# A six-layer attention stack and a quantised feed-forward on one core: the steady order of all five queues written anew, implied waits dropped, filler products dropped

## The chip, the cores and the metric

One core of a Trainium2 chip runs the whole program in one launch. The metric is the device time in microseconds (us); three runs of the kernel before gave 1197.34, 1201.46 and 1201.83, median 1201.46.

## What is computed

The input is x, eight sequences of 1024 rows of 128. For each sequence b, six vectors come from a condition vector: `mod = silu(c) @ wmod`, split into sa, ca, ga, sb, cb, gb.

```
h = layernorm(x) * (1 + ca) + sa
for i in range(6):                      # the attention stack, h is its x
    xn = layernorm(x, ln1)
    q = softmax(xn @ wq, head dim); k = softmax(xn @ wk, rows); v = xn @ wv
    x = (q @ (k.T @ v)) @ wo + bo + x   # linear attention, 8 heads of 16
    xn = layernorm(x, ln2)
    x = leaky_relu(xn @ w1) @ w2 + x    # hidden width 512
x = x + ga * h
x = x + gb * fp4_ffn(layernorm(x) * (1 + cb) + sb)   # inner width 352
```

`fp4_ffn` rounds inputs and weights in blocks of 16 to the values of a 4-bit float and computes `silu(gate) * up` and the down product. All is float32.

## The kernel before

**Items.** An item is one sequence in one layer: 48 items, number i, layer i // 8. A sequence's 1024 rows lie as 128 partitions x 8 tiles of 128. Per item TensorE does product_k (4 products of 512 columns, fp32, line 556), product_q (16 of 128 columns, fp32, line 568), product_z (k against the normalised rows, 16 fp32, line 577), context and context_out (2 fp32 each, lines 585 and 591), attend (16 fp32, line 598), eight first_mlp pieces (each three float16 products of 512 columns, lines 612 to 614: high x high, low x high, high x low), and eight second_mlp pieces (each twelve float16 products of 128 columns, lines 627 to 629). In the record an fp32 product shows as two passes; the counts here are of passes.

**Who does what.** ACT (ScalarE) takes the hidden pieces out of PSUM (copy_hidden, line 880), splits them into high halves (line 889), scales the normalised rows (lines 850 and 861) and does the exponentials. DVE (VectorE) does statistics (lines 1097 and 1103), softmax maxima and sums, 32x32 block transposes (lines 1184, 1198, 1207) and the additions into x_all. POOL (GpSimd) does the low halves (hidden_low, line 1785; second_norm_low, line 1777), the roots and part of the scaling. SP (SyncE) issues every DMA of the loop: round trips through DRAM that finish the transposes of n, q and k (send_..., fetch_...), and turn_hi and turn_lo (lines 331 and 336), two DMA transposes that bring the split rows of item i into norm2_hi and norm2_lo, which the first_mlp pieces of item i read.

**One buffer.** norm2_hi and norm2_lo exist once. So turn_hi(i) and turn_lo(i) wait `hidden_done >= PIECES * i`: all eight first_mlp pieces of item i - 1 must be over. first_mlp(i, 0) waits for the landing of both. Between the last piece of item i - 1 and the first piece of item i lies what TensorE does in the meantime.

**Orders.** Each engine runs a function `items(v)` for v = 0, 1, 2, ...; a line `if on(v - 4): first_mlp(v - 4, 6)` means that in step v the engine does this piece of item v - 4. The engines' queues are in order, so these lists, written out by hand, are the schedule; semaphores only hold it together. Lines with `v == n` are the opening (weights are folded and split, the first items are transposed by TensorE) and the start of the feed-forward, whose units (16 of half a sequence) begin in steps 48 to 53 and then run in `ffn_phase`. `round_weights` and `prepare_gates` are one extra DVE operation in each of steps 10 to 26 and 27 to 44. `keep_warm` (line 522) is TensorE's filler in steps 0 to 3: products of 256 columns that nobody reads.

Of the kernel before, what the change touches and what calls it, by code (L numbers as in the profile page):

```python
# [37 lines left out]
def adaln_block(nc, x, ln1_w, ln1_b, wq, wk, wv, wo, bo, ln2_w, ln2_b, w1, w2,  # L38
# [31 lines left out]
    with ctx:  # L70
# [208 lines left out]
        def _(sp):  # L279
# [143 lines left out]
            for v in range(ITEMS + 3):  # L423
                items(v)
# [24 lines left out]
        def _(pe):  # L449
# [99 lines left out]
            def product_k(i):  # L549

                pe.wait_ge(norm1_t_ready, i + 1)
                pe.wait_ge(wk_ready, 16 * (i // B + 1))
                w = wk_s[:, i // B % 2 * D:i // B % 2 * D + D]
                after(pe, ctx_o_ready, i - 1)
# [5 lines left out]
            def product_q(i):  # L560

                pe.wait_ge(norm1_t_ready, i + 1)
                pe.wait_ge(wq_ready, 16 * (i // B + 1))
                after(pe, q_shifted, i)
# [16 lines left out]
            def context(i):  # L581
                pe.wait_ge(z_t_ready, i + 1)
                pe.wait_ge(wv_ready, 16 * (i // B + 1))
# [3 lines left out]
            def context_out(i):  # L587
                pe.wait_ge(ctx_t_ready, i + 1)
                pe.wait_ge(wo_ready, 16 * (i // B + 1))
# [11 lines left out]
            def first_mlp(i, n):  # L601
# [14 lines left out]
            def second_mlp(i, t):  # L616
# [3 lines left out]
                if t % TH == 0:  # L620
                    pe.wait_ge(weights_ready, 2 * DEPTH)
                    pe.wait_ge(hidden_lo_ready, 2 * i + h + 1)
                    after(pe, x_ready, 2 * (i - 1) + h + 1)
# [37 lines left out]
            def product_gate(u, t):  # L661
                pe.wait_ge(f_x_q_t_ready, u + 1)
# [4 lines left out]
            def product_up(u, t):  # L667
                pe.wait_ge(f_x_q_t_ready, u + 1)
# [4 lines left out]
            def turn_hidden(u, t):  # L673
                if u == 0:
                    pe.wait_ge(x_ready, 2 * ITEMS - 1)
                pe.wait_ge(f_hid_q_ready, u + 1)
# [7 lines left out]
            def product_down(u):  # L684
# [3 lines left out]
                pe.wait_ge(f_x1_ready, u + 1)  # L688
# [29 lines left out]
            def items(v):  # L718
                if v == 0: turned_bias_rows()
                if v == 0: hidden_bias_cols()  # L720
                if v == 0: output_bias_rows()
                if v == 0: keep_warm(mlp0_bank, 18)
                if v == 0: turn_first_n(0)
                if on(v - 2): context_out(v - 2)
                if v == 2: keep_warm(mlp0_bank, 10)
                if v == 3: keep_warm(mlp0_bank, 16)
                if on(v - 4): first_mlp(v - 4, 6)
                if on(v - 4): first_mlp(v - 4, 7)
# [1216 lines left out]
```

## Time and profile before

| | |
|---|---|
| median of three runs | 1201.46 us |
| the profiled execution | 1198.31 us |
| its span in the trace | 1196.6 us |
| busy of the span: PE, POOL, DVE, ACT | 94%, 91%, 90%, 87% |
| instructions | 30119 |
| fillers, line 522 | 172 products, 22 us busy |

A share of busy time is a mean over three stages: the opening (to about 160 us), the steady items, and the feed-forward at the end (from about 970 us). PE's busy time has modelled ends: for TensorE read the distance from one start to the next. The row PEclk gives the granted clock, 9 or 1.00 being the full 2.4 GHz and half of it 1.2 GHz.

### The profile page before, as it was taken

What the parts mean: (1) busy time and instruction counts of PE and PEld (TensorE: products, weight loads), DVE (VectorE), ACT (ScalarE), POOL (GpSimd) and SP (SyncE); (2) the same over time, 40 slices, a digit from 0 to 9 for tenths busy, and PEclk for the clock granted to TensorE, in tenths of its full rate; (3) what the DMA queues carried; (4) which work ended last, traced back from release to release, by engine and by line L of the source; (5) the groups of instructions that cost most, each with busy time, mean ns of one, the idle gap of its engine ahead of it and who ended that gap; (6) DMA issues with size and microseconds to landing.
All of it is one profiled execution on the core that took longest, in us unless ns stands there. A gap on an engine that the chain in (4) does not pass through costs nothing.

```text
span 1196.6 us, 30119 instructions
## 1 busy us (share of the span) xinstructions
PE 1130.7 (94%) x9722; PEld 865.7 (72%) x9722; DVE 1074.4 (90%) x2885; ACT 1035.2 (87%) x1776; POOL 1091.4 (91%) x920
## 2 busy tenths in 40 slices
PE   7787999999999999999999999999999988999996
PEld 5575777777777777777778777777787755565664
DVE  7899989989999999999999999999987589999972
ACT  5687999999999999999999999999999886767662
POOL 4889999999999999999999999999999988999762
PEclk8798999999999999999999999999999999999998
DMA  8121877777667776687776776766777420110000
GB/s 308 36 71 53 234 187 224 195 195 223 193 195 214 196 216 194 180 224 187 216 201 197 216 206 183 221 190 204 208 193 218 108 71 18 36 37 36 18 19 36
DMA packets 213864, 190.22 MB, mean 159 GB/s; under 512 B 113392, under 2 KB 192080, under 8 KB 213712
## 3 DMA queue, kind: packets, MB, share of 16 engines
q1 hardware_dynamic: 213712, 188.31, 55.3%
q8 instruction: 81, 1.33, 0.5%
q14 instruction: 71, 0.58, 0.2%
HBM read 87.06 MB, written 76.02 MB: 136 GB/s over the span
## 4 chain that ended last, share of the span: by engine, by line
PE 50%; POOL 24%; issue 15%; DVE 6%; ACT 2%; DMA 1%; SPq 1%; DVEq 0%; POOLq 0%; ACTq 0%
POOL hidden L1785 10%; POOL rows_split L1777 4%; PE pair_mlp L556 4%; PE pair_mlp L577 4%; PE pair L598 4%; PE pair L568 4%; PE ring_pair L612 3%; PE ring_pair L614 3%; PE ring_pair L613 3%; PE mlp L696 3%; PE pair_mlp L670 3%; POOL arena L1758 2%; POOL arena L1791 2%; PE pair_mlp L681 2%; PE mlp L629 2%
## 5 line engine op out<-in xcount | busy, mean ns | idle before, releaser
L1785 POOL TENSOR_TENSOR hidden<-hidden 128x2048 f16<-128x2048 f32 x92 | 376.3, 4090 | 0.0
L880 ACT ACTIVATE hidden<-ring_pair,hidden_bias 128x512 f32<-128x512 f32 x384 | 245.6, 686 | 26.1 <-PE ring_pair L614 26.0
L889 ACT ACTIVATE hidden<-hidden 128x2048 f16<-128x2048 f32 x96 | 183.3, 1909 | 19.9 <-PE mlp L629 16.1
L1097 DVE BATCH_NORM_STATS2 bn<-x_all 128x6 f32<-128x128 f32 x896 | 184.2, 278 | 5.3 <-POOL x_all L1737 2.0
L1711 POOL TENSOR_TENSOR rstd<-ve,minus_half 128x8 f32<-128x8 f32 x104 | 170.7, 1641 | 0.0
L850 ACT ACTIVATE arena<-x_all,nmr,rstd 128x128 f32<-128x128 f32 x384 | 157.7, 494 | 0.0
L612 PE MATMUL ring_pair<-arena,halves 128*128 128x512 f16 x384 | 146.0, 380 | 3.4 <-ACT hidden L880 1.7
L614 PE MATMUL ring_pair<-arena,halves 128*128 128x512 f16 x384 | 146.0, 380 | 0.0
L613 PE MATMUL ring_pair<-arena,halves 128*128 128x512 f16 x384 | 146.0, 380 | 0.0
L627 PE MATMUL mlp<-halves,hidden 128*128 128x128 f16 x768 | 135.9, 219 | 1.4 <-issue 1.4
L627 PE MATMUL pair_mlp<-halves,hidden 128*128 128x128 f16 x768 | 136.0, 219 | 0.0
L628 PE MATMUL pair_mlp<-halves,hidden 128*128 128x128 f16 x768 | 136.0, 219 | 0.0
L629 PE MATMUL pair_mlp<-halves,hidden 128*128 128x128 f16 x768 | 136.0, 219 | 0.0
L629 PE MATMUL mlp<-halves,hidden 128*128 128x128 f16 x768 | 135.9, 219 | 0.0
L628 PE MATMUL mlp<-halves,hidden 128*128 128x128 f16 x768 | 135.9, 219 | 0.0
L1777 POOL TENSOR_TENSOR rows_split<-arena,rows_split 128x1024 f16<-128x1024 f32 x48 | 103.9, 2164 | 0.3 <-ACT rows_split L870 0.3
L598 PEld LDWEIGHTS pair<-small,arena 128*128 128x128 f32 x768 | 95.1, 195 | 10.6 <-DVE small L1241 4.2
L1791 POOL TENSOR_TENSOR arena<-arena,q_rec 128x1024 f32<-128x1024 f32 x48 | 93.9, 1956 | 6.9 <-DVE q_rec L1177 6.4
L598 PE MATMUL pair<-small,arena 128*128 128x128 f32 x768 | 95.9, 279 | 3.0 <-DVE small L1241 3.0
L861 ACT ACTIVATE arena<-x_all,nmr,rstd 128x128 f32<-128x128 f32 x240 | 97.8, 498 | 1.1 <-POOL nmr L1750 1.1
L556 PE MATMUL pair_mlp<-arena,layer_w 128*128 128x512 f32 x192 | 96.2, 624 | 1.4 <-ACT arena L811 1.4
L577 PE MATMUL pair_mlp<-arena 128*128 128x128 f32 x752 | 94.3, 279 | 3.0 <-DMA arena<-k_away 2.7
(206 smaller groups left out, 3144.5 us busy)
## 6 DMA issues: line engine op xcount, KB each, us to landing
n_away<-all_blocks SPq DMA_DIRECT2D x47, 512.0 KB, 3.0
norm_raw<-n_away SPq DMA_DIRECT2D x188, 128.0 KB, 3.2
k_away<-all_blocks SPq DMA_DIRECT2D x45, 512.0 KB, 2.8
q_away<-all_blocks SPq DMA_DIRECT2D x45, 512.0 KB, 3.3
arena<-k_away SPq DMA_DIRECT2D x180, 128.0 KB, 3.5
arena<-q_away SPq DMA_DIRECT2D x180, 128.0 KB, 3.6
x_all<-in_L_attn_x SPq DMA_DIRECT2D x8, 512.0 KB, 5.5
x_in<-in_L_attn_x SPq DMA_DIRECT2D x8, 512.0 KB, 4.0
```

The costliest lines, as they stand in the source:

```text
L598: last = nc.tensor.matmul(tile(S0, t), tile(q_prob_t, t), ctx_o, start=True, stop=True)
L612: nc.tensor.matmul(ring[n % 2], hi, rows_hi, start=True, stop=False)
L613: nc.tensor.matmul(ring[n % 2], lo, rows_hi, start=False, stop=False)
L614: nc.tensor.matmul(ring[n % 2], hi, rows_lo, start=False, stop=True).then_inc(hidden_done, 1)
L627: nc.tensor.matmul(o, rows_hi, hi, start=(c == 0), stop=False)
L628: nc.tensor.matmul(o, rows_hi, lo, start=False, stop=False)
L629: last = nc.tensor.matmul(o, rows_lo, hi, start=False, stop=(c == HC - 1))
L880: act.activation(hidden_t[:, c * W + h * HALF:c * W + (h + 1) * HALF], ring[n % 2], ACT.Prelu, bias=hidden_bias[:, b:b + 1], scale=HIDDEN_ ...
L889: act.activation(half_rows(hidden_hi, h), half_rows(hidden_t, h), ACT.Copy).then_inc(hidden_hi_ready, 1)
L1097: last = nc.vector.bn_stats(bn[:, 6 * t:6 * t + 6], src(t))
L1711: return pool.tensor_tensor(rstd[:, 0:tiles], ve[:, 0:tiles], minus_half[:, 0:tiles], ALU.pow).then_inc(rstd_ready, 1)
L1785: pool.tensor_tensor(half_rows(hidden_lo, h), half_rows(hidden_t, h), half_rows(hidden_hi, h), ALU.subtract).then_inc(hidden_lo_ready, 1)
```

## The change

Nothing that is computed for the output changes. Four things do:

1. The lists of all five engines are ordered anew. On TensorE the fp32 groups product_z, context, context_out, product_k and product_q now stand right behind a first_mlp piece (512-column products); attend stands behind second_mlp(v - 5, 7). product_z and context move from item v - 1 to v - 2, first_mlp pieces 0 to 5 from item v - 3 to v - 4, and second_mlp 0 to 4 from item v - 4 to v - 5. In the new list the pieces follow each other so: second_mlp 0 to 3; first 0; z; first 1, 2; context; second 4, 5; first 3; context_out; second 6, 7; attend; first 4, 5; k; first 6, 7; q; and then the next step.
2. Waits that another wait already implies are left out: on TensorE those for the weights (kept where a layer or the stage begins), for norm2 in pieces 1 to 7, and a few on buffers; on ACT k_done, ln_ready, scales_ready; on DVE ln_ready and bo_ready.
3. All keep_warm calls are gone.
4. The opening and the feed-forward's start are placed anew in the lists.

```diff
@@ SP
             def items(v):
+                if on(v - 3): fetch_q(v - 3)
+                if on(v - 1): fetch_n(v - 1)
+                if on(v - 2): send_k(v - 2)
+                if on(v - 2): fetch_k(v - 2)
                 if on(v - 2): send_q(v - 2)
-                if on(v - 2): fetch_k(v - 2)
+                if on(v - 4): turn_hi(v - 4)
+                if on(v - 4): turn_lo(v - 4)
                 if on(v): send_n(v)
-                if on(v - 2): fetch_q(v - 2)
-                if on(v): fetch_n(v)
-                if on(v - 1): send_k(v - 1)
-                if on(v - 3): turn_hi(v - 3)
-                if on(v - 3): turn_lo(v - 3)
@@ TensorE, first_mlp
-                pe.wait_ge(weights_ready, DEPTH)
-                pe.wait_ge(norm2_hi_ready, 16 * (i + 1))
-                pe.wait_ge(norm2_lo_ready, 16 * (i + 1))
+                if i == 0 and n == 0:
+                    pe.wait_ge(weights_ready, DEPTH)
+                if n == 0:
+                    pe.wait_ge(norm2_hi_ready, 16 * (i + 1))
+                    pe.wait_ge(norm2_lo_ready, 16 * (i + 1))
@@ TensorE, the order: before (steady lines only)
-                if on(v - 2): context_out(v - 2)
-                if on(v - 4): first_mlp(v - 4, 6)
-                if on(v - 4): first_mlp(v - 4, 7)
-                if on(v - 2): attend(v - 2)
-                if on(v - 5): second_mlp(v - 5, 5)
-                if on(v - 5): second_mlp(v - 5, 6)
-                if on(v): product_k(v)
-                if on(v - 5): second_mlp(v - 5, 7)
-                if on(v): product_q(v)
-                if on(v - 3): first_mlp(v - 3, 0)
-                if on(v - 3): first_mlp(v - 3, 1)
-                if on(v - 4): second_mlp(v - 4, 0)
-                if on(v - 3): first_mlp(v - 3, 2)
-                if on(v - 3): first_mlp(v - 3, 3)
-                if on(v - 4): second_mlp(v - 4, 1)
-                if on(v - 4): second_mlp(v - 4, 2)
-                if on(v - 1): product_z(v - 1)
-                if on(v - 3): first_mlp(v - 3, 4)
-                if on(v - 3): first_mlp(v - 3, 5)
-                if on(v - 1): context(v - 1)
-                if on(v - 4): second_mlp(v - 4, 3)
-                if on(v - 4): second_mlp(v - 4, 4)
@@ TensorE, the order: after
+                if on(v - 5): second_mlp(v - 5, 0)
...
+                if on(v - 5): second_mlp(v - 5, 3)
+                if on(v - 4): first_mlp(v - 4, 0)
+                if on(v - 2): product_z(v - 2)
+                if on(v - 4): first_mlp(v - 4, 1)
+                if on(v - 4): first_mlp(v - 4, 2)
+                if on(v - 2): context(v - 2)
+                if on(v - 5): second_mlp(v - 5, 4)
+                if on(v - 5): second_mlp(v - 5, 5)
+                if on(v - 4): first_mlp(v - 4, 3)
+                if on(v - 2): context_out(v - 2)
+                if on(v - 5): second_mlp(v - 5, 6)
+                if on(v - 5): second_mlp(v - 5, 7)
+                if on(v - 2): attend(v - 2)
+                if on(v - 4): first_mlp(v - 4, 4)
+                if on(v - 4): first_mlp(v - 4, 5)
+                if on(v): product_k(v)
+                if on(v - 4): first_mlp(v - 4, 6)
+                if on(v - 4): first_mlp(v - 4, 7)
+                if on(v): product_q(v)
```

The steady lists of two more engines after the change, in a row, with v left out (so "-3" is item v - 3):

- DVE: inverse_q -3, mask_context -4, block_k -3, inverse_k -3, add_mlp -7 half 0, bias_context -4, then the one extra operation of the step (round_weights or prepare_gates; before, it stood between moments1 and affine_z), add_mlp -7 half 1, block_q -3, add_attention -4, bn2_rows -4, moments2 -4, block_n -1, max_k -2, max_q -2, shift_q -2, bn1_rows 0, moments1 0, affine_z -3, sum_q -2.
- POOL: second_norm_low -5, hidden_low -6 half 0, root2 -4, hidden_low -6 half 1, root1 0, normalise_q -2, normalise1 0.

## Rows read from the trace of the kernel before

**Rows 1.** Windows view: busy time by engine, steady stretch; columns start:end, length, busy (count).
```profile
300.00:960.00 660.00, 656.15 (x6307) 515.51 (x6304) 608.53 (x1674) 625.70 (x999) 646.95 (x529) 1.00 0.71 197
```

**Rows 2.** Timeline of PE over one item: start, us, instruction, count.
```profile
602.40 1.94 PE L556 MATMUL pair_mlp<-arena,layer_w 128*128 128x512 f32 x4
604.18 0.22 PE L627 MATMUL mlp<-halves,hidden 128*128 128x128 f16 x1
604.85 2.00 PE L568 MATMUL pair<-layer_w,arena 128*128 128x128 f32 x16
606.69 0.38 PE L612 MATMUL ring_pair<-arena,halves 128*128 128x512 f16 x1
...
617.57 1.95 PE L598 MATMUL pair<-small,arena 128*128 128x128 f32 x16
619.35 0.22 PE L627 MATMUL mlp<-halves,hidden 128*128 128x128 f16 x1
620.69 1.94 PE L556 MATMUL pair_mlp<-arena,layer_w 128*128 128x512 f32 x4
...
624.97 0.38 PE L612 MATMUL ring_pair<-arena,halves 128*128 128x512 f16 x1
```

**Rows 3.** Timeline of PE, opening: a product_k and a product_q behind 512-column or fp32 work.
```profile
75.09 1.88 PE L556 MATMUL pair_mlp<-arena,layer_w 128*128 128x512 f32 x4
76.81 1.95 PE L568 MATMUL pair<-layer_w,arena 128*128 128x128 f32 x16
```

**Rows 4.** Timeline of POOL: the low half of the norm in two following items.
```profile
839.08 2.14 POOL L1777 TENSOR_TENSOR rows_split<-arena,rows_split 128x1024 f16<-128x1024 f32 x1
857.12 2.14 POOL L1777 TENSOR_TENSOR rows_split<-arena,rows_split 128x1024 f16<-128x1024 f32 x1
```

**Rows 5.** Timeline of PE: starts of first_mlp and attend around the transposes.
```profile
162.36 0.38 PE L612 MATMUL ring_pair<-arena,halves 128*128 128x512 f16 x1
...
936.19 0.38 PE L612 MATMUL ring_pair<-arena,halves 128*128 128x512 f16 x1 [1.61 <-DMA arena<-rows_split]
...
947.05 1.95 PE L598 MATMUL pair<-small,arena 128*128 128x128 f32 x16
```

**Rows 6.** Timeline of SP: issues of turn_hi (L331) and turn_lo (L336).
```profile
175.79 1.46 SPq L331 DMA_TRANSPOSE arena<-rows_split  x1
177.34 2.69 SPq L336 DMA_TRANSPOSE arena<-rows_split  x1
...
912.58 1.42 SPq L331 DMA_TRANSPOSE arena<-rows_split  x1
914.09 1.27 SPq L336 DMA_TRANSPOSE arena<-rows_split  x1
...
933.00 1.26 SPq L336 DMA_TRANSPOSE arena<-rows_split  x1
947.29 1.24 SPq L331 DMA_TRANSPOSE arena<-rows_split  x1
948.63 1.26 SPq L336 DMA_TRANSPOSE arena<-rows_split  x1
```

**Rows 7.** Source view, L336: issue to landing; 42 items (160:940), then that of 948.63.
```profile
DMA to landing us min/median/max: 2.8/2.9/4.9
...
DMA to landing us min/median/max: 2.7/2.7/2.7
```

**Rows 8.** DMA view, 175:183, then 160:940: packets, MB, share.
```profile
q8 instruction: 1, 0.02, 0.8%
...
q8 instruction: 62, 1.02, 0.6%
```

**Rows 9.** Chain that ended last, by line: windows 0:60 and 60:120.
```profile
by line: PE mlp L510 15.0%; PE ring_pair L471 12.4%; PE pair_mlp L556 9.5%; PE pair L463 6.3%; issue 6.1%; PE pair_mlp L522 6.0%; DVE bn L1097 5.3%; PE ring_pair L499 4.6%; PE pair_mlp L463 3.3%; DMA arena<-in_L_c 2.6%; PE ring_pair L491 2.
by line: issue 26.4%; POOL x_all L1734 11.6%; POOL x_all L1737 8.7%; POOL rows_split L1777 8.5%; PE pair_mlp L522 5.5%; POOL arena L1791 4.9%; POOL arena L1758 4.5%; POOL rstd L1711 3.0%; PE pair L598 3.0%; PE pair L568 3.0%; DVE bn L1097 2
```

**Rows 10.** Timeline of PE: an attend at half clock in the opening.
```profile
118.38 3.78 PE L598 MATMUL pair<-small,arena 128*128 128x128 f32 x16 [0.93 <-DVE small L1241]
```

More of the change, by code:

```diff
@@ L421, in items @@
                 if 46 <= v < 46 + 2: load_back(v - 46)
-            for v in range(ITEMS + 3):
+            for v in range(ITEMS + 4):
                 items(v)
@@ new lines, in items @@
+                if on(v - 5): second_mlp(v - 5, 1)
+                if on(v - 5): second_mlp(v - 5, 2)
+                if on(v - 5): second_mlp(v - 5, 3)
+                if v == 51: product_gate(0, 0)
+                if v == 51: product_up(0, 0)
+                if v == 52: product_up(1, 0)
+                if v == 52: product_gate(1, 1)
+                if v == 52: product_up(1, 1)
+                if v == 52: product_gate(1, 2)
+                if v == 52: product_up(1, 2)
+                if on(v - 4): first_mlp(v - 4, 0)
@@ L875, in copy_hidden @@
                 act.wait_ge(hidden_done, PIECES * i + n + 1)
-                act.wait_ge(scales_ready, 1)
+                if i == 0 and n == 0:
+                    act.wait_ge(scales_ready, 1)
                 if c == 0:
@@ new lines, in items @@
+                if v == 2: front_hat(4)
+                if v == 3: front_hat(5)
+                if v == 3: copy_q(0)
+                if v == 49: x_epsilon(0)
+                if on(v - 4): normalise2(v - 4, 1)
+                if v == 4: copy_k(2)
+                if v == 51: x_ties(0)
+                if on(v - 5): copy_hidden(v - 5, 1)
+                if v == 52: gate(0, 1)
+                if on(v - 4): second_norm_high(v - 4)
+                if v == 4: front_hat(6)
+                if on(v - 1): first_norm_t(v - 1)
@@ L1047, in items @@
+                if v == 3: copy_q(1)
+                if v == 3: prepare_weights(1, range(0, 3))
+                if v == 4: copy_q(2)
+                if v == 4: front_hat(7)
+                if on(v - 5): copy_hidden(v - 5, 6)
+                if v == 52: gate(0, 3)
+                if on(v - 5): copy_hidden(v - 5, 7)
                 if v == 51: rows_turned(0)
                 if v == 52: rows_turned(1)
-                if on(v - 5): copy_hidden(v - 5, 6)
-                if on(v - 5): copy_hidden(v - 5, 7)
@@ new lines, in items @@
+                if v == 52: x_scaled(0)
+                if v == 52: x_shifted(0)
+                if v == 52: x_moments(2)
+                if v == 52: x_max(0)
+                if v == 52: x_scale(0)
+                if v == 52: x_inverse(0)
+                if v == 52: x_lift(0)
+                if v == 52: x_lower(0)
+                if v == 52: hidden_low(46, 0)
+                if v == 52: x_rows(3)
+                if v == 52: x_scaled(1)
+                if v == 52: x_shifted(1)
+                if v == 52: x_moments(3)
@@ new lines, in items @@
+                if v == 52: x_max(1)
+                if v == 53: x_rows(4)
+                if v == 53: hidden_tile(0, 1)
+                if v == 53: x_scaled(2)
+                if v == 54: hidden_scale(1)
+                if v == 54: x_lift(3)
+                if v == 54: hidden_inverse(1)
+                if v == 54: x_lower(3)
+                if v == 54: hidden_tile(2, 0)
+                if on(v - 4): bias_context(v - 4)
+                if v == 4: front_stats(6)
+                if v == 5: front_stats(7)
@@ L1574, in items @@
+                if v == 6: prepare_weights(1, range(3, DEPTH))
+                if 10 <= v < 10 + W_STEPS: round_weights(v - 10)
+                if 27 <= v < 27 + GATE_STEPS: prepare_gates(v - 27)
+                if on(v - 7): add_mlp(v - 7, 1)
+                if v == 52: x_scale(1)
+                if v == 52: x_inverse(1)
+                if v == 52: hidden_low(46, 1)
                 if v == 52: x_lift(1)
```

311 lines of the change are left out of this document (123 added, 188 removed).

## The prediction, made before the result was known

> **What bounds the kernel now.** I read the page's busy row and its 40 slices first: from about 160 to 970 us every slice of PE is at 9, so the steady items decide. The windows view of 300 to 960 then says that more than PE is full: of 660 us PE is busy 656, POOL 647, ACT 626, DVE 609 [rows 1]. The timeline of PE gives the period: product_k of one item starts at 602.40, that of the next at 620.69, 18.29 us [rows 2]; over 42 items, from the first piece of item 3 at 162.36 to that of item 45 at 936.19, it is 773.8 / 42 = 18.42 us [rows 5]. The timeline of POOL shows what POOL needs by itself: 857.12 - 839.08 = 18.04 us between the same operation of two items [rows 4]. Last I read the timeline of SP and the landings of the two DMA transposes, because they stand between the first_mlp pieces of one item and those of the next.
>
> **What the order is worth on TensorE alone.** In rows 2 a product_q group takes 606.69 - 604.85 = 1.84 us behind a 128-column product, and product_k 604.18 - 602.40 = 1.78. Behind wide or fp32 work product_k takes 76.81 - 75.09 = 1.72 [rows 3]; attend, already behind a 512-column piece, takes 619.35 - 617.57 = 1.78 for as many passes as product_q [rows 2]. So a group that follows a short product pays about 0.055 us: its first weights aren't there. Before, four groups of an item pay (k, q, z, context_out); after, attend alone. That is 3 x 0.055 = 0.16 us an item, and if nothing else bound, 18.27 - 0.16 = 18.11 us, just above POOL's 18.04 (18.27 is the undisturbed period; the 0.15 between it and 18.42 are waits in some items, which would go too). 42 x (18.42 - 18.11) = 13 us would be the gain.
>
> **What the order costs.** turn_hi(i) may be issued only when piece 7 of item i - 1 is over, and piece 0 of item i waits until turn_hi(i) and turn_lo(i) have landed. Before, that path has the time of attend, three second_mlp, product_k and product_q beside it: 624.97 - 617.57 = 7.40 us [rows 2]. After, only product_q (1.79 behind a long product) and second_mlp 0 to 3. Two second_mlp pieces take 620.69 - 619.35 = 1.34 [rows 2], four 2.68. Together 4.47 us.
>
> What the path needs, step by step, with no other traffic: piece 7 ends and attend starts at 947.05, turn_hi is issued at 947.29 (0.24), turn_lo at 948.63 (1.34), and lands 2.7 later [rows 5 to 7]. From the landing to the first product it takes 936.19 - (933.00 + 2.9) = 0.3 [rows 5, 6]. Sum 4.6. With the loop's traffic turn_lo follows at 914.09 - 912.58 = 1.51 and lands after 2.9, the median [rows 6, 7]: 0.24 + 1.51 + 2.9 + 0.3 = 4.95, I take 4.9. Both are over 4.47, so TensorE waits at piece 0 in every item. This wait is in a ring: piece 0 to piece 7 is the rest of the period, 18.11 - 4.47 = 13.64 us of TensorE's own work, so the period can't be under 13.64 + 4.6 = 18.2, and is 13.64 + 4.9 = 18.54 in an ordinary item.
>
> Not every item is ordinary. turn_lo's landing reaches 4.9 us [rows 7]; asked one by one, 12 of the 42 items take over 5.5 us from turn_hi's issue to the last landing, the first at 175.79 and the last at 912.58 [rows 6] (the first: 177.34 + 4.9 - 175.79 = 6.4), on average 6.0 against 4.4 in the others' quiet ones. In the first of them a DMA packet of queue q8, kind instruction, 16 KB, falls into the window [rows 8]; the other eleven have one within 4 us of the issue too, and the quiet ones don't. There are 62 of them over these 42 items, 1.5 an item: TensorE's program being fetched, in front of the transposes on one of the DMA engines. Before the change 7.40 us hide that. After it each such item waits 1.6 more. With the same share, 12 / 42 x 1.6 = 0.46, the mean period is 18.54 + 0.46 = 19.0. Bounds: 18.2 (no fetch ever in the way, no traffic) and 19.5 (the stretch of the program that runs between piece 7 and piece 0 now holds 128 instructions in 4.5 us where it held fewer per us, so six in ten may be hit). I take 19.0, the value of the rows. Steady stretch: 42 x (19.0 - 18.42) = +24 us, between 42 x (18.2 - 18.42) = -9 and +45.
>
> Here the Trainium skill says otherwise (Runtime: NRT & Kernel Launch, section Instruction fetch mechanics): the program is fetched in blocks of 16 KiB by the sequencer's own DMA queue, and crossing a block's end costs one tail-bump that is mostly hidden. The block size agrees with the packet in rows 8; that the fetch costs nothing is taken up as the second rival. The skill's DMA: Bandwidth & Descriptors, section Latency and other measured facts, gives 261 GB/s for DMA transposes; two of 256 KB would by that estimate take 2 us and fit beside 4.47. The measured 4.6 from rows 5 to 7 decides against it, because issue and landing count too.
>
> **The other queues.** In the new order the chains through the other engines have room. DVE, with 609 of 660 busy [rows 1], loses the wait at context_out; its extra operation no longer stands between product_z and context, where it now costs up to 0.3 in alternate items; that saving is inside the ring's new bound and not counted again. SP: turn_hi waits on SP's queue for piece 7 and behind it stand send_n, fetch_q, fetch_n and send_k; these have between 2 and 6 us to spare before their readers. POOL's floor 18.04 is below 19.0. So none of them is late next; the price if I am wrong is the difference of their floors to 19.0, nothing.
>
> **Implied waits.** They are instructions on queues that don't bind, 24 on TensorE in an item before and hidden under its running products. Worth 0; at most the 1.4 us that PE is idle with nothing to wait for. They shorten TensorE's program by a few per cent, and so the number of fetches.
>
> **The opening.** The fillers are 6.0% and 5.5% of the chain in 0:60 and 60:120, 3.6 + 3.3 = 6.9 us [rows 9]; that is the most that their going gives. Against it: without them TensorE is idle more and the clock lower. An attend at half clock takes 3.78 instead of 1.95 [rows 10, 2]; the five fp32 groups of an item then cost some 8 us more, 24 for items 0 to 2 if all lay on the chain, of which I take 4. And the pipeline is deeper: piece 0 of an item comes 3 periods + 4.3 us after its product_k before (three periods, and 606.69 - 602.40 [rows 2]), and 4 periods - 10.6 after (piece 0 to product_k is 10.6 in the new list), with 18.3 that is 3.4 later. Sum -6.9 + 4 + 3.4 = +0.5; ends -7 and +20.
>
> **The end.** In items 46 and 47 there is no product_q, so 2.68 us lie beside the transposes' 4.6: 2 us of waiting each, where 7.4 were planned; TensorE has holes there anyway. I take +2 (ends -3 and +5). The feed-forward's phases themselves are unchanged.
>
> **Sum.** 1198.3 (the profiled execution) + 24 + 0.5 + 2 = 1225. The profiled execution was 3 us below the median of 1201.46; by the middle of that, 1227.
>
> **Rivals.**
> - *The transposes fit.* If the path from piece 7 to piece 0 takes 4.47 or less in the new surroundings (the sends now stand elsewhere), TensorE's own bound of 18.11 holds and nothing waits: -13 steady, -5 opening, 1183. For it: all else was seen to have room. Against it: no item in the trace does it in under 4.57. It decides from 4.47 us on. This is the one on the other side.
> - *Fetches cost nothing*, by the rule above: they fall where TensorE doesn't wait. Period 18.54: +5 steady, +2.5, 1207. For it: the places of fetches shift with the program's length. Against it: 12 of 42.
> - *A ring through DVE or POOL stays the bound* at 18.3 to 18.6 with the transposes at their best: 1200. For it: POOL 98% busy [rows 1]. Against it: POOL's 18.04.
> - *A cold opening*: the forecast, and 12 us more because the clock stays at half until item 3: 1238.
>
> **Chances.** Forecast 0.53, the transposes fit 0.14, fetches free 0.14, another ring 0.09, cold opening 0.10. 0.5% (6 us) is about what a measurement of this kernel can tell from no change. Faster: the first rival and a little of the third, 0.16. Same: most of the third and a third of the second, 0.14. Slower: 0.70. The range leaves most of the first rival out below and reaches the cold opening above: 1191 to 1246; the likeliest case's own is 1214 to 1240.
>
> **What would show it.** In the trace after: PE idle before line 612, once an item, released by DMA arena<-rows_split, in total 20 us or more (1.6 before); from one piece 0 to the next near 19.0; turn_hi issued 0.24 after piece 7 ends; products k, q, z and context_out 0.055 shorter; line 522 absent and PEclk lower before 130 us. I am wrong if that idle is under 5 us and the period under 18.3. If the period is right and the total isn't, look at the opening.

## The result, and the profile after

The changed kernel takes 1218.34 us (median of 4, 1217.96 to 1221.04), the kernel before 1201.09 (median of 4, 1197.34 to 1201.83): ratio 1.0158, 95% interval 1.0142 to 1.0175: slower by 1.6%, clear of the noise. The forecast was 1227 in 1191 to 1246, slower. The direction and the place were right; only half of the mechanism was.

The windows view of the same stretch as [rows 1]. PE, POOL, ACT and DVE have all become less busy (PE from 656 to 639 us of 660): nothing took over as the bound by being full; TensorE waits.

```profile
300.00:960.00 660.00, 639.32 (x6135) 509.09 (x6134) 584.44 (x1629) 613.34 (x970) 628.28 (x515) 1.00 0.68 197
```

The timeline of PE over two periods, cut to the starts that matter: product_q (L567) starts when piece 7 has given up its place, and the next L615 is piece 0 of the following item, behind four second_mlp.

```profile
613.37 1.95 PE L567 MATMUL pair<-layer_w,arena 128*128 128x128 f32 x16
615.56 0.23 PE L631 MATMUL pair_mlp<-halves,hidden 128*128 128x128 f16 x1 [0.24 <-POOL hidden L1777]
...
619.33 0.38 PE L615 MATMUL ring_pair<-arena,halves 128*128 128x512 f16 x1 [0.92 <-issue]
...
632.97 1.95 PE L567 MATMUL pair<-layer_w,arena 128*128 128x128 f32 x16
637.43 0.38 PE L615 MATMUL ring_pair<-arena,halves 128*128 128x512 f16 x1
...
651.07 1.95 PE L567 MATMUL pair<-layer_w,arena 128*128 128x128 f32 x16
655.54 0.38 PE L615 MATMUL ring_pair<-arena,halves 128*128 128x512 f16 x1
```

The timeline of SP around the same three turns (queue, line, what is issued), and then, from the source view of L336 over 613.5:618 and 633:637.5, its landings:

```profile
613.61 1.25 SPq L331 DMA_TRANSPOSE arena<-rows_split  x1
614.95 1.25 SPq L336 DMA_TRANSPOSE arena<-rows_split  x1
616.30 0.53 SPq L316 DMA_DIRECT2D n_away<-all_blocks  x1
...
633.21 1.24 SPq L331 DMA_TRANSPOSE arena<-rows_split  x1
634.54 1.26 SPq L336 DMA_TRANSPOSE arena<-rows_split  x1
...
651.31 1.24 SPq L331 DMA_TRANSPOSE arena<-rows_split  x1
652.64 1.26 SPq L336 DMA_TRANSPOSE arena<-rows_split  x1
654.00 0.53 SPq L316 DMA_DIRECT2D n_away<-all_blocks  x1
```

```profile
DMA to landing us min/median/max: 4.3/4.3/4.3
...
DMA to landing us min/median/max: 2.8/2.8/2.8
```

From 632.97 and from 651.07 it is 4.46 and 4.47 us to piece 0: exactly the cover, TensorE waits for nothing, and 651.07 - 632.97 = 18.10 us is the undisturbed period. The path fits because it is shorter than predicted: 0.24, then 1.33 to turn_lo's issue, 2.8 to its landing. In the turn at 613.37 the landing takes 4.3, and TensorE is idle 0.92 us in front of piece 0. A q8 packet (the record's kind is instruction) stands in that window of the DMA view and in neither of the other two:

```profile
q8 instruction: 1, 0.02, 1.4%
```

The waits view of 200:950, the engines first, then SP's queue alone (who waited, for whom: us in total, times, longest). Before, over the same stretch, the same view gave 1.2 us in 4 times for ScalarE's wait for the norm's rows (the second line here) and no wait in front of DVE's block_n (the first).

```profile
DVE all_blocks L1190 <- issue: 41.7, 36, 3.1
ACT arena L810 <- DMA norm_raw<-n_away: 37.8, 33, 3.2
PEld ring_pair L615 <- ACT hidden L873: 22.1, 54, 1.3
POOL hidden L1777 <- ACT hidden L882: 19.9, 21, 2.5
...
PE ring_pair L615 <- issue: 10.8, 10, 1.7
...
PEld pair_mlp L631 <- POOL hidden L1777: 6.7, 15, 0.5
...
SPq L80 <- PE ring_pair L617: 99.6, 39, 3.0
```

This holds the half that I had not predicted. ScalarE waits 37.8 us for the norm's DMA (norm_raw) in front of first_norm_t, and SyncE stands 99.6 us in turn_hi's wait for piece 7 (L80 is the helper `after`). In the kernel before, SyncE's queue stood instead in front of send_n:

```profile
SPq L316 <- DVE all_blocks L1198: 59.5, 36, 2.4
...
SPq L80 <- PE ring_pair L614: 7.6, 1, 7.6
```

So send_n was issued the moment its data was there (0.03 us behind the end of block_n on DVE, which makes its data; median of items 8 to 43); now it stands behind both transposes and goes 1.30 us late. With a slower landing as well, first_norm_t starts 10.0 us behind block_n, where it was 8.9. The timeline of ACT shows who pays: the two copies of hidden pieces (L873) that TensorE's first_mlp and POOL's hidden_low live on stand behind the wait.

```profile
642.01 1.05 ACT L862 ACTIVATE rows_split<-arena 128x1024 f16<-128x1024 f32 x1
644.09 1.24 ACT L810 ACTIVATE arena<-norm_raw,ln_cols 128x1024 f32<-128x1024 f32 x1 [1.02 <-DMA norm_raw<-n_away]
645.23 1.25 ACT L873 ACTIVATE hidden<-ring_pair,hidden_bias 128x512 f32<-128x512 f32 x2
```

**The norm's loop.** These waits close into a loop: first_norm_t of item i stands on ScalarE in front of normalise1 of item i + 1, block_n (DVE) waits for normalise1, send_n and fetch_n take its rows to DRAM and back, and first_norm_t of item i + 1 waits for them. Its steps, by the start, end and landing times of the traces, are means of items 8 to 43 in us. They add up to the period in every kernel, since the loop comes round once an item; what tells is where it has slack, and where it has none any delay in it is passed on to the next item:

| step | before | after | e8 | e9 | e14 |
|---|---|---|---|---|---|
| first_norm_t's start to normalise1's end (ScalarE) | 6.12 | 7.45 | 7.41 | 6.17 | 8.08 |
| to block_n's start | 2.16 | 0.09 | 0.09 | 0.11 | 0.09 |
| block_n | 1.23 | 1.25 | 1.25 | 1.24 | 1.25 |
| to send_n's issue | 0.05 | 1.27 | 1.42 | 2.17 | 0.04 |
| to its landing | 3.22 | 3.55 | 3.46 | 3.52 | 3.37 |
| to fetch_n's last landing | 4.99 | 5.17 | 5.25 | 5.24 | 5.39 |
| to first_norm_t's start | 0.65 | 0.06 | 0.05 | 0.07 | 0.41 |
| sum | 18.42 | 18.84 | 18.93 | 18.52 | 18.63 |

Before, 2.8 us of the loop are slack (2.16 and 0.65). After, all of it is gone: block_n starts 0.09 behind normalise1, first_norm_t 0.02 behind the landing in the median, and ScalarE is idle 0.02 in its stretch. Send_n's delay took 1.2 of it. ScalarE's own order took 1.3: two copies of hidden pieces more stand between first_norm_t and normalise1 than before (four instead of two, 0.65 each). Slower landings took 0.5. The 1.27 in front of send_n is in part TensorE's doing, since turn_hi ahead of it waits for piece 7; without it the loop would need 17.6, under TensorE's 18.10 (an estimate from the column). (e8, e9 and e14 are explained under Experiments; e14's 8.08 has 0.5 of idle in it.)

**Where the 19.9 us of the two profiled executions are** (spans 1196.6 and 1216.5; the medians lie 17.3 apart): piece 0 of item 3 starts at 165.78 instead of 162.36 (+3.4); the 42 items to item 45 take 18.86 us each instead of 18.42 (+18.4); from there to item 47's +0.5; the rest -2.5.

**What TensorE waits for.** I took for items 4 to 45 what each step from one start to the next has over its undisturbed length (0.216 us for a 512-column product, 0.056 in second_mlp, 0.112 and 0.429 in the fp32 groups), and put it down to the function that started late, in us an item. This tells where TensorE waited; it doesn't tell what the time would be without that wait, since another one can take its place:

| kernel | period | piece 0 | other pieces | second_mlp | fp32 groups |
|---|---|---|---|---|---|
| before | 18.42 | 0.05 | 0 | 0 | 0.40 |
| after | 18.86 | 0.37 | 0.20 | 0.25 | 0.05 |
| e1 piece 7 earlier | 18.85 | 0.10 | 0.65 | 0.05 | 0.06 |
| e2 no turn_lo | 18.34 | 0 | 0.08 | 0.23 | 0.05 |
| e3 norm later | 18.71 | 0.50 | 0.05 | 0.13 | 0.05 |
| e7 shorter cover | 19.37 | 1.03 | 0.07 | 0.12 | 0.18 |
| e8 halves | 18.91 | 0.03 | 0.47 | 0.35 | 0.06 |
| e9 halves, norm later | 18.51 | 0.04 | 0.15 | 0.24 | 0.10 |
| e14 halves, send first | 18.64 | 0.06 | 0.01 | 0.03 | 0.58 |
| e11 halves, send first, norm later | 18.70 | 0.06 | 0.03 | 0.04 | 0.61 |
| e15 fetch_q first | 19.07 | 0 | 0.56 | 0.37 | 0.15 |

### The profile page after: what moved, and what is told of

It is laid out like the page before. It is cut to its first block, busy times and chain, and to the rows that moved or that the text cites. A ratio compares the mean times of both kernels' runs of the same rounds, so it can differ in the third digit from the quotient of the medians.

```text
span 1216.5 us, 28237 instructions
## 1 busy us (share of the span) xinstructions
PE 1115.7 (92%) x9550; PEld 858.4 (71%) x9550; DVE 1060.9 (87%) x2885; ACT 1039.3 (85%) x1776; POOL 1084.9 (89%) x920
## 3 DMA queue, kind: packets, MB, share of 16 engines
q8 instruction: 76, 1.25, 0.4%
## 4 chain that ended last, share of the span: by engine, by line
PE 43%; DVE 11%; ACT 11%; issue 10%; SPq 8%; DMA 8%; POOL 5%; DVEq 0%; ACTq 0%; POOLq 0%
DMA norm_raw<-n_away 5%; PE pair L599 5%; PE pair_mlp L556 5%; PE ring_pair L615 4%; PE ring_pair L617 4%; PE ring_pair L616 4%; ACT hidden L873 4%; POOL hidden L1777 3%; PE pair_mlp L576 3%; DMA n_away<-all_blocks 2%; PE pair L567 2%; SPq L331 2%; PE mlp L633 2%; PE mlp L632 2%; PE mlp L631 2%
## 5 line engine op out<-in xcount | busy, mean ns | idle before, releaser
L873 ACT ACTIVATE hidden<-ring_pair,hidden_bias 128x512 f32<-128x512 f32 x384 | 245.7, 675 | 12.4 <-PE ring_pair L617 12.0
L615 PE MATMUL ring_pair<-arena,halves 128*128 128x512 f16 x384 | 146.4, 381 | 26.9 <-issue 13.8
L842 ACT ACTIVATE arena<-x_all,nmr,rstd 128x128 f32<-128x128 f32 x384 | 157.2, 483 | 3.4 <-POOL nmr L1764 3.2
L631 PE MATMUL pair_mlp<-halves,hidden 128*128 128x128 f16 x768 | 132.9, 221 | 6.7 <-POOL hidden L1777 6.2
L632 PE MATMUL mlp<-halves,hidden 128*128 128x128 f16 x768 | 134.2, 219 | 0.0
L633 PE MATMUL mlp<-halves,hidden 128*128 128x128 f16 x768 | 134.2, 219 | 0.0
L631 PE MATMUL mlp<-halves,hidden 128*128 128x128 f16 x768 | 134.2, 219 | 0.0
L633 PE MATMUL pair_mlp<-halves,hidden 128*128 128x128 f16 x768 | 132.7, 220 | 0.0
L632 PE MATMUL pair_mlp<-halves,hidden 128*128 128x128 f16 x768 | 132.7, 220 | 0.0
L599 PE MATMUL pair<-small,arena 128*128 128x128 f32 x768 | 99.4, 284 | 4.6 <-DVE small L1234 4.6
L576 PEld LDWEIGHTS pair_mlp<-arena 128*128 128x128 f32 x752 | 92.7, 195 | 12.1 <-issue 5.7
L567 PEld LDWEIGHTS pair<-layer_w,arena 128*128 128x128 f32 x768 | 94.7, 194 | 8.9 <-issue 2.5
L1190 DVE STREAM_TRANSPOSE all_blocks<-arena 128x1024 f32<-128x1024 f32 x47 | 58.4, 1243 | 46.7 <-issue 46.5
```

The lines of the kernel that those rows point to most:

```text
L576: last = nc.tensor.matmul(S1[:, 0:D], tile(norm1[i % NB], t), tile(first_k[i % 2], t) if i < FIRST else rows[:, t], start=(t == 0), stop=( ...
L615: nc.tensor.matmul(ring[n % 2], hi, rows_hi, start=True, stop=False)
L631: nc.tensor.matmul(o, rows_hi, hi, start=(c == 0), stop=False)
L632: nc.tensor.matmul(o, rows_hi, lo, start=False, stop=False)
L633: last = nc.tensor.matmul(o, rows_lo, hi, start=False, stop=(c == HC - 1))
L873: act.activation(hidden_t[:, c * W + h * HALF:c * W + (h + 1) * HALF], ring[n % 2], ACT.Prelu, bias=hidden_bias[:, b:b + 1], scale=HIDDEN_ ...
```

## Experiments

Ratios are to the kernel before, run beside each on the same chip.

**The ring of the transposes.** Four kernels change the cover, the path, or free ScalarE.

*e7, the cover cut by one second_mlp:*

```diff
-                if on(v - 5): second_mlp(v - 5, 3)
...
                 if on(v - 4): first_mlp(v - 4, 1)
                 if v == 51: product_gate(0, 1)
+                if on(v - 5): second_mlp(v - 5, 3)
```

> The changed kernel with one edit on TensorE: second_mlp(v - 5, 3) moves from before piece 0 to before piece 2. Cover between piece 7 and piece 0 falls from 4.47 to 3.80 us, the order of the fp32 groups stays. Ring theory: the quiet path (0.24 + 1.33 + 2.75 + 0.09 = 4.41 us) no longer fits, every item waits 0.6 us more at piece 0: period 19.4, 1235 to 1248 us. Rival (another queue paces): 1218 us.

Measured 1254.3 us, ratio 1.0443 [1.0422, 1.0464]. The cover went from 4.47 to 3.80 and the waits at piece 0 from 0.37 to 1.03 us an item. By rows: an undisturbed path needs 0.24 + 4.12 + 0.09 = 4.45, so 0.65 in each item, and 1.2 more in the 16 of 42 that are disturbed (0.46) give 1.11. The ring and its price stand. The period (19.37) is the expected 19.4; the time is above the expected 1235 to 1248, because the profile also has 5.4 us more before piece 0 of item 3 and 6.4 more between those of items 45 and 47.

*e1, piece 7 issued earlier on TensorE (pieces 4 and 5 before attend, 6 and 7 behind it, then k and q):*

```diff
-                if on(v - 2): attend(v - 2)
                 if on(v - 4): first_mlp(v - 4, 4)
                 if on(v - 4): first_mlp(v - 4, 5)
-                if on(v): product_k(v)
+                if on(v - 2): attend(v - 2)
                 if on(v - 4): first_mlp(v - 4, 6)
                 if on(v - 4): first_mlp(v - 4, 7)
+                if on(v): product_k(v)
```

> The changed kernel with one edit on TensorE: pieces 4 and 5 stand before attend, 6 and 7 right behind it, then product_k and product_q. Between piece 7 and the next piece 0 stand now product_k, product_q and four second_mlp, 1.72 us more (6.19 instead of 4.47 us), and attend follows a 512-column piece. Theory (the ring piece 7 - two transposes - piece 0 costs, made long by TensorE's program fetches): the waits at piece 0 (0.37 us an item after the change) go, the delays behind them shrink, and the period falls from 18.86 to 18.2 to 18.45 us: 1192 to 1201 us. Rival (the first-norm transposes come late on ACT and set the pace, the transposes at piece 0 only seem to): 1214 to 1218 us, only attend's 0.055 us is gained.

Measured 1223.07, ratio 1.0198 [1.0174, 1.0221]: a miss. Piece 0's waits fell as expected, to 0.10, and those of later pieces rose to 0.65. The waits view names a new place, attend's reader:

```profile
DVE x_all L1241 <- PE pair L599: 67.0, 39, 5.5
PEld ring_pair L615 <- ACT hidden L873: 43.9, 112, 2.7
ACT arena L830 <- DVE cols L1148: 28.3, 40, 2.0
```

Attend is 1.3 us later in the item, DVE waits for it with block_n and max_k behind it, and ScalarE's exp_k and copies wait for DVE. It freed one ring and closed another, so it tells nothing on the size of the first. It also shows that a prompt send_n isn't enough: block_n to send_n is 0.03 us here.

*e2, turn_lo issued for item 0 only. The low half of the norm isn't turned after that; this part of the computation is left out:*

```diff
             def turn_lo(i):
+                if i > 0:
+                    return
```

> The changed kernel without turn_lo for items 1 to 47: the low halves of the rows are not brought over, so the third product of each first_mlp piece reads item 0's. One transpose instead of two lies between piece 7 and piece 0: 0.24 + about 2.8 to 3.4 + 0.09 us against 4.47 us of cover; a fetch in the way adds 1.6 and just about fits. Ring theory: the 0.37 us an item at piece 0 nearly goes, and some of the later waits: 1195 to 1204 us. Rival (another queue paces): 1215 to 1218 us.

Measured 1199.6, ratio 0.9986 [0.9972, 0.9999]. As expected (1195 to 1204). Piece 0 waits for nothing and the period is 18.34, not 18.1: second_mlp still starts 0.23 late, so a third of the loss (0.24 of 0.76) is left. With one transpose less on SyncE's queue send_n is late by 0.42 instead of 1.30 us, so this kernel eases the norm's loop too and doesn't separate the two.

*e3, first_norm_t behind copy_hidden 3 on ScalarE:*

```diff
-                if on(v - 1): first_norm_t(v - 1)
                 if on(v - 5): copy_hidden(v - 5, 2)
                 if on(v - 5): copy_hidden(v - 5, 3)
+                if on(v - 1): first_norm_t(v - 1)
```

> The changed kernel with one edit on ACT: first_norm_t(v - 1) moves from before copy_hidden 2 to behind copy_hidden 3, 1.3 us later. ACT waited there 41.8 us in all for norm_raw, and what is behind it (copies of pieces 2 and 3, the high half, and through it POOL's hidden_low and second_mlp) was late. Theory (0.20 us an item at later first_mlp pieces and 0.25 at second_mlp are this wait passed on): 5 to 17 us less, 1201 to 1213 us, while the waits at piece 0 stay near 0.37 us. Rival (those waits too come only from the transposes' delays at piece 0): 1216 to 1220 us.

Measured 1215.11, ratio 1.0114 [1.0092, 1.0137]: by the ratios 0.44% less than the changed kernel (some 5 us), by the medians 3.2 us, just outside the expected 1201 to 1213. The waits at second_mlp and later pieces fell from 0.46 to 0.18 together, piece 0's rose from 0.37 to 0.50: what ScalarE gives back, the transposes take.

**Both rings at once.** e8 splits each transpose into halves of 512 columns; the half for pieces 0 to 3 waits for piece 3 only, so that the ring through piece 0 is open and all the work is done.

```diff
-            def turn_hi(i):
+            def turn_hi(i, h):
                 sp.wait_ge(rows_hi_ready, i + 1)
-                after(sp, hidden_done, PIECES * i)
+                after(sp, hidden_done, PIECES * (i - 1) + HC * (h + 1))
...
+                if on(v - 4): turn_hi(v - 4, 0)
+                if on(v - 4): turn_lo(v - 4, 0)
+                if on(v - 4): turn_hi(v - 4, 1)
+                if on(v - 4): turn_lo(v - 4, 1)
                 if on(v): send_n(v)
```

> The changed kernel, with each of the two DMA transposes of an item split into its two halves of 512 columns: the half that pieces 0 to 3 read may go as soon as piece 3 of the item before is over, the other once piece 7 is. All arithmetic stays. Theory (the ring piece 7 of one item, transposes, piece 0 of the next): the transposes that piece 0 needs can now start some 8 us before piece 7 ends, so the waits at piece 0 (0.37 us an item) go, and what is left are the 0.25 before second_mlp and 0.20 before later pieces: period 18.3 to 18.5, 1196 to 1204 us, about what the kernel without turn_lo showed (1199.6), this time with all the work. First rival (four issues of 1.3 us on SyncE's queue instead of two delay the sends and fetches behind them, and with them first_norm_t): waits move to k and second_mlp, 1208 to 1220. Second rival (piece 0's waits weren't the cause, others take their place at once): 1215 to 1222.

Measured 1225.34, ratio 1.0209 [1.0190, 1.0227]. Of the theory only the part on piece 0 held (0.03 us); the first rival's mechanism gave the time, at a higher price than its 1208 to 1220. send_n is 1.33 us late, as it was before the split: now because of four issues, since SyncE's wait for TensorE's pieces (L80) is down from 99.6 to 0.4 us. ScalarE waits longer, and the other pieces and second_mlp pay 0.82. So the open ring bought nothing: the norm's loop has no slack in this kernel either.

```profile
ACT arena L815 <- DMA norm_raw<-n_away: 46.8, 32, 3.3
PEld ring_pair L620 <- ACT hidden L879: 33.8, 100, 0.7
POOL hidden L1784 <- ACT hidden L888: 26.2, 26, 2.3
```

*e9, as e8 with e3's move:*

```diff
-                if on(v - 1): first_norm_t(v - 1)
...
                 if on(v - 5): copy_hidden(v - 5, 3)
+                if on(v - 1): first_norm_t(v - 1)
```

> As the kernel with the transposes in halves, and on ScalarE first_norm_t moved behind copy_hidden 3, so that ScalarE's copies of the first pieces don't stand behind its wait for the norm's DMA. Theory: the two waits are separate. In the changed kernel the move alone took second_mlp's waits from 0.25 to 0.13 an item and later pieces' from 0.20 to 0.05, while piece 0's rose to 0.50; with piece 0 free, both gains show: period 18.2 to 18.3, 1190 to 1197 us. Rival (one ring only, the second wait is a shadow of the first): no difference between the two kernels of this call, within 2 us.

Measured 1205.84, ratio 1.0046 [1.0029, 1.0063]: 19.5 us less than e8 from the place of one instruction on ScalarE, where the same move gave 3.2 (by the ratios 5) with the first ring closed. Neither ring alone is the cause. In the norm's loop the move takes 1.24 off ScalarE's stretch and send_n loses 0.75 of it again on SyncE's queue. The theory's direction held, its size (1190 to 1197) didn't: ScalarE still waits 29.3 us in 29 times in the new place.

*e14, as e8, but send_n leaves before the second halves, and fetch_n before fetch_q:*

```diff
+                if on(v - 1): fetch_n(v - 1)
                 if on(v - 3): fetch_q(v - 3)
-                if on(v - 1): fetch_n(v - 1)
...
                 if on(v - 4): turn_hi(v - 4, 0)
                 if on(v - 4): turn_lo(v - 4, 0)
+                if on(v): send_n(v)
                 if on(v - 4): turn_hi(v - 4, 1)
                 if on(v - 4): turn_lo(v - 4, 1)
-                if on(v): send_n(v)
```

> The changed kernel with the transposes in halves as in e8, and on SyncE's queue send_n moved ahead of the second halves and fetch_n ahead of fetch_q; ScalarE's order as changed. Theory (a second ring, by way of SyncE's order: in the changed kernel send_n stands behind turn_hi and turn_lo, is issued 1.30 us after its data is ready where it was 0.03 before, and first_norm_t comes 10.0 us behind block_n instead of 8.9; ScalarE waits 0.9 us for it each item with the copies of hidden pieces behind that): block_n to send_n falls under 0.3 us, ScalarE's wait before first_norm_t under 0.3, the waits at first_mlp and second_mlp (0.47 and 0.35 in e8) under half of that, period 18.2 to 18.4, 1195 to 1206 us. Rival (the norm's rows are late because their values are, not because of the queue; the copies would wait anyway): 1220 to 1226 as e8.

Measured 1218.03, ratio 1.0157 [1.0129, 1.0184], against 1195 to 1206. The mechanism is there: send_n is back at 0.03 us behind block_n, first_norm_t at 8.9, the norm's loop has slack again (0.4, and 0.5 of idle on ScalarE), and the waits at pieces and second_mlp fell from 0.82 to 0.04. How much of that fall send_n alone gave isn't shown: fetch_n moved too, and TensorE now waits 0.52 at attend, which gives the other engines time. That wait made the time miss, since fetch_q comes later: attend starts 3.5 us behind fetch_q's last issue (6.7 in the changed kernel), and in 25 of 40 items 0.09 us behind its landing (3.2 in the median, up to 5.2).

```profile
PE pair L604 <- issue: 14.3, 16, 2.6
ACT arena L815 <- DMA norm_raw<-n_away: 13.1, 15, 2.9
```

*e11, e14 with first_norm_t behind copy_hidden 3 as well:*

```diff
                 if on(v - 5): copy_hidden(v - 5, 3)
+                if on(v - 1): first_norm_t(v - 1)
```

> As e14, and first_norm_t behind copy_hidden 3 on ScalarE as in e9 (1205.8 us). Theory: both rings are open then, what is left is TensorE's own 18.05 and POOL's 18.04 a period with small waits, 18.15 to 18.3, 1189 to 1198 us: faster than the kernel before (1200). Rival (e9 has already taken all that the norm's lateness cost, and its rest is a chain through POOL's hidden_low and ScalarE's hidden_high): 1203 to 1208 as e9.

Measured 1218.68, ratio 1.0154 [1.0132, 1.0176]: as e14, and a miss for theory and rival. Attend waits in this kernel as in e14, so it doesn't tell what the place of first_norm_t is worth without that wait.

*e15, e11 with fetch_q first again and the second halves behind fetch_n:*

```diff
                 if on(v - 3): fetch_q(v - 3)
                 if on(v - 1): fetch_n(v - 1)
+                if on(v - 5): turn_hi(v - 5, 1)
+                if on(v - 5): turn_lo(v - 5, 1)
```

> As e11 (halves; send_n ahead of the second halves; first_norm_t behind copy_hidden 3), but fetch_q is again ahead of fetch_n and the second halves stand behind fetch_n. In e11 the waits at the pieces were gone (0.055, 0.035 and 0.030 us an item) and 0.56 stood at attend instead, which starts 3.7 us after fetch_q's last issue where it starts 6.7 after it in the changed kernel; a second half is needed 10.9 us after its issue and has room. Theory (attend waits for q's landing, which e11's own order made late): attend back to 0.05, period 18.15 to 18.3, 1190 to 1198 us, faster than the kernel before (1200). Rival (once TensorE stops waiting at attend, a chain through POOL's hidden_low, 18.04 a period, and ScalarE takes the time back): waits at second_mlp again, period 18.5, 1203 to 1208 as e9.

Measured 1232.73, ratio 1.0290 [1.0246, 1.0333]. Attend is back at 0.05 as expected, and I had overlooked another reader of the transposes' landing: second_norm_high (L868) may write the next rows only when the last half has gone.

```profile
ACT rows_split L868 <- DMA arena<-rows_split: 60.0, 39, 4.0
```

I had looked for room in front of TensorE's piece 4 only (5.3 us behind the issue of the last half, enough). The norm's loop has 3.1 us of slack in front of first_norm_t here, so it isn't what sets this time. None of the kernels that do all the work beats the one before.

**Opening and waits.** *e12, the kernel before with the implied waits left out on all engines:*

```diff
-                pe.wait_ge(wk_ready, 16 * (i // B + 1))
+                if i % B == 0:
+                    pe.wait_ge(wk_ready, 16 * (i // B + 1))
...
-                after(pe, ctx_o_ready, i - 1)
```

> The kernel before with the implied waits left out on all engines and nothing else: its orders, fillers and transposes as before. Theory, as predicted: the waits were hidden under running work, 1198 to 1203 us, period within 0.05 of 18.42. Rival (the sequencers' time counts, and fewer instructions mean fewer fetches): 1190 to 1197.

Measured 1199.68, ratio 1.0001 [0.9984, 1.0018], period 18.41: nothing, as predicted.

*e6, the kernel before with no keep_warm:*

```diff
-                if v == 0: keep_warm(mlp0_bank, 18)
...
-                if v == 1: keep_warm(mlp0_bank, 20)
```

> The kernel before with all keep_warm products left out (nothing reads them), its order and waits untouched. Theory, as predicted: -6.9 us of filler work on the chain and some +4 from the lower clock, so 1195 to 1200 us. Rival (the fillers lie beside the wait for the first layers' data and cost nothing, while the clock falls without them): 1202 to 1208, the loss before piece 0 of item 3. Steady period unchanged at 18.42 in both.

Measured 1201.51, ratio 1.0008 [0.9992, 1.0024], between theory and rival, the period 18.46. Windows view, 30:60, the kernel before and then e6 (after the engines: granted clock, DMA share, GB/s):

```profile
30.00:60.00 30.00, 21.73 (x116) 16.07 (x117) 24.13 (x87) 19.40 (x41) 24.79 (x28) 0.78 0.11 36
```

```profile
30.00:60.00 30.00, 13.90 (x57) 10.02 (x58) 27.29 (x91) 20.05 (x42) 25.40 (x29) 0.67 0.10 36
```

TensorE drops from 21.7 to 13.9 us of work and its clock from 0.78 to 0.67, and piece 0 of item 3 starts at 162.05 instead of 162.36: cost and gain of the fillers together are nothing there.

*e5, the changed kernel with fillers put back:*

```diff
                 if v == 0: output_bias_rows()
...
+                if v == 0: keep_warm(mlp0_bank, 30)
+                if v == 1: keep_warm(mlp0_bank, 20)
```

> The changed kernel with keep_warm back in the opening (18 before turn_first_n at v = 0, then 30, 20, 20 and 14 behind output_bias_rows at v = 0 to 3; nothing reads them). Theory (the opening's 3.4 us come from the deeper pipeline, and the fillers' price and the clock they buy about cancel): 1214 to 1221 us, piece 0 of item 3 within 2 us of 165.8. Rival (cold opening: the missing fillers are what costs): granted clock in 30 to 130 us goes up, piece 0 of item 3 at 162 or before, 1210 to 1214. Third (the fillers are pure cost): 1220 to 1226.

Measured 1228.02, ratio 1.0223 [1.0203, 1.0243]. In this order they are a pure cost of some 8 us (0.65% over the changed kernel's ratio), the third case's direction and a little beyond it; piece 0 of item 3 starts at 175.9 in its profile, that of a run 7 us above its median, with a period of 19.00. The granted clock did rise, from 0.68 to 0.75 in 30 to 60 us.

## Why the prediction was right, and where it wasn't

- *What bounds the kernel, the ring.* Right that it is there: 0.67 us less cover costs 0.66 at piece 0 (e7), the ring opened leaves 0.03 (e8). Wrong that it alone sets the period: with it open the period is 18.91 (e8), not 18.1.
- *The gain on TensorE alone.* Right: the groups k, q, z and context_out start without the 0.05 they paid, and the undisturbed period is 18.10 (forecast 18.11).
- *The ordinary item's path.* The term of 4.9 us was too large. I took issue gap (1.51) and landing (2.9) from items whose transposes had other traffic beside them [rows 6, 7] (the median gap of the 42 was even 1.76); where turn_hi now stands they are 1.33 and 2.75, what the quiet rows at 947 to 951 had shown. The wake-up, which I took as 0.3, is 0.09. Sum 4.41 against a cover of 4.47. So the ordinary item doesn't wait, and the rival *the transposes fit* is true of it; it fails as a forecast of the time because of the rest.
- *The fetches.* Right in kind and near in size. Over items 4 to 45 the time from turn_hi's issue to the last landing is 4.10 us in 25 items and 5.30 in the 17 others, 1.2 more (forecast 1.6, in 12; the 1.6 compared the 12 with the quietest items at 4.4, where the other 30 have 4.6 on average, which would have been 1.4). 13 of the 17 have a q8 packet between 0.5 and 4.0 us behind the issue; of the 25 two have one, at 3.8 and 3.9. The other four (items 4, 8, 11 and 45, 4.5 to 4.8 us) have an 8 KB packet of a second queue of kind instruction, q14, 1.5 to 3.5 us behind the issue; none of the 25 has one between 1.0 and 3.9. 17/42 x 1.2 = 0.49 is the ceiling, 0.37 the measured wait. The rival *fetches cost nothing* falls by this coincidence in time; no run takes the packets away. The Trainium skill (Runtime: NRT & Kernel Launch, Instruction fetch mechanics) calls the cost of crossing a block's end mostly hidden. The 7.40 us of cover before hid it; the 0.06 us of room here don't.
- *The other queues.* This step failed: "send_n, fetch_q, fetch_n and send_k; these have between 2 and 6 us to spare before their readers". I looked at TensorE's reader, product_k, which indeed has 2.7 us, and not at the engine in between: first_norm_t had 0.65 us behind the landing in the kernel before, and stands on ScalarE in front of copies that have no room and of normalise1, which feeds the next send_n. The loop of the norm had 2.8 us of slack in all; 1.2 us on SyncE's queue and 1.3 from ScalarE's new order, which the prediction didn't look at, used it up, so that late landings in the loop lengthen the period, which they didn't before. In TensorE's waits that is 0.46 us an item, of which e3's move alone took 0.28 away; that send_n's delay gives the rest is argued from e14 and the loop, not shown by a run of its own. The rival *a ring through DVE or POOL* came nearest to this, with the wrong engines: the loop goes through ScalarE, DVE and SyncE.
- *The sum.* 0.37 + 0.46 + 0.05 over an own work of 17.98 (18.05 in an item, less the one of the 42 without product_k and product_q) is 18.86; I had 19.0 with 0.9 at piece 0 alone. Two errors, 0.5 too much there and 0.46 overlooked, met. That the period came out near is luck. The range was right, the sign to look for, line 612 idle for 20 us or more with a period near 19.0, half right: the idle was 15.6 (42 x 0.37).
- *Implied waits.* Right for the old order, nothing (e12). In the new order something hangs on them: the wake-up is 0.25 in the kernel before and in e6 (five items of each, those whose piece 0 waits for the landing), with two more wait instructions of 0.05 us on TensorE's queue behind the landing, and 0.09 in e12 and the changed kernel. With 0.16 more the ordinary path would be 4.57, over the cover of 4.47: an estimate from these numbers, not run. By it the second part of the change is what makes the ordinary item fit.
- *The opening.* The terms for fillers and clock, -6.9 and +4 or -2.9 together, aren't confirmed: together they measured +1 in the old order (e6, interval -1 to +3), and with fillers put back the new order loses 8 (e5, in other places of the list). No run separates the two terms. The total, +3.4, equals my term for the deeper pipeline, but that isn't shown: the kernel without implied waits has 166.91 for the same start in the old order, and the kernels in the new order without fillers have 165.8 to 171.2, so single profiles differ by as much.
- *The end.* -2.5 instead of +2. Behind piece 0 of item 47 the kernel before has 227.2 us, the changed one 224.7. The waits' going doesn't explain it: e12, without them, has 225.0, but e6, with all of them, 225.9, and e8, without, 226.5. The cause stays open.

Not run is the plainest test, the changed kernel with send_n alone moved in front of turn_hi, or with the two copies back behind normalise1. Open is also whether a version exists that keeps the undisturbed 18.10 in every item. It would need send_n and fetch_q prompt, the transposes of both halves landed before second_norm_high, and all on one queue; e8, e14 and e15 each gave up one of the three.

## What to carry to other kernels

When instructions are reordered on a queue that issues DMAs, follow each one behind the new wait to its reader, and ask what stands behind that reader on its own engine; the reader's own deadline isn't the one that counts. Where a transfer feeds its own next turn through several engines, add up that loop with its slack, before and after: here it had 2.8 us of slack, and the two places where it stood looked harmless, since nobody waited there. Take durations for a moved transfer from rows with the traffic of its new place. A ring that fits by a twentieth of a microsecond is closed by the first disturbed transfer: count how often one is, and leave that much room.

## What I had not expected of the hardware

- TensorE's first product follows the semaphore of a landed DMA transpose by 0.09 us at the least (piece 0 in items 4 to 45), and by 0.25 in the kernel before, where two more wait instructions stand in between (0.05 us each, starting 0.11 apart).
- A DMA transpose (128x1024 f16) lands 2.7 to 2.8 us after its issue, and after 4.3 with one 16 KB instruction packet in the window. An 8 KB packet of the other instruction queue goes with 0.4 to 0.7 us more.
- At a granted clock of 0.67 instead of 0.78 in 30 to 60 us the opening took as long: with 13.9 us of TensorE's work in 30 there was room for slower products.
